# Every engine's loops written out in a transformer block with two routed FFN passes and one attention: constant waits, no branches

## The reference

```python
x = x + 0.5 * ffn(layernorm(x))
x = x + attn(layernorm(x))
x = x + 0.5 * ffn(layernorm(x))
```

## The kernel before, in words

| sequence | engines | before the loop | loop | behind it |
|---|---|---|---|---|
| s0 of a pass, 8 blocks | PE, ACT, DVE, SP | 1 | 3 times 2 | 1 |
| s1, 8 blocks | PE, ACT | 2 | 3 times 2 | 0 |
| s1, 8 blocks | SP | 1 | 3 times 2 | 1 |
| e, 16 blocks | PE, ACT, DVE, SP | 1 | 3 times 4 | 3 |
| attention, 38 steps | PE, ACT, DVE, POOL | 7 | 6 times 4 | 7 |
| layer norm, 8 blocks | POOL | 1 | 3 times 2 | 1 |
| scatter, 32 tiles | POOL | 3 | 14 times 2 | 1 |
| expert sums, 16 blocks | POOL | 1 | 3 times 4 | 3 |

## Time and profile before

### The profile page before, as it was taken

The page is one execution under the profiler, slowest core; times in us unless marked ns, Lnnn a source line. Parts: engine busy times, 40 slices in busy tenths (PEclk is TensorE's granted clock), DMA queues, the critical chain, the costliest instruction groups (busy, mean ns, idle before and its releaser), DMA issues. The chain is left out here.

```text
span 2445.0 us, 42873 instructions
## 1 busy us (share of the span) xinstructions
PE 2300.4 (94%) x14276; PEld 2116.3 (87%) x14276; DVE 1379.4 (56%) x2890; ACT 970.2 (40%) x1940; POOL 501.5 (21%) x614
## 2 busy tenths in 40 slices
PE   7999999998999997788888988999999998999997
PEld 6888888887999997688888877888888887999997
DVE  4554454433666666778777773554454433666663
ACT  3333333332444444545444542333333332544442
POOL 1000003442121122223222220000003443121222
PEclk9999999998999999778787787999999998999999
DMA  6212113422343443100000002212113422343441
GB/s 207 72 59 87 61 57 107 126 81 72 94 104 91 99 99 90 61 1 0 0 0 0 0 1 87 76 56 87 61 57 109 124 80 68 98 103 89 102 92 17
DMA packets 198241, 175.59 MB, mean 72 GB/s; under 512 B 18697, under 2 KB 176829, under 8 KB 198144
## 3 DMA queue, kind: packets, MB, share of 16 engines
q1 hardware_dynamic: 177152, 144.57, 19.4%
q0 software_dynamic: 20992, 29.77, 6.4%
HBM read 108.51 MB, written 72.26 MB: 74 GB/s over the span
## 5 line engine op out<-in xcount | busy, mean ns | idle before, releaser
L340 PE MATMUL gate_p<-zh,w 128*128 128x320 f32 (+1 forms) x2048 | 641.3, 358 | 3.3 <-DVE zl L845 3.3
L340 PE MATMUL quad<-zh,w 128*128 128x320 f32 (+1 forms) x2048 | 628.8, 352 | 0.0
L1032 DVE TENSOR_TENSOR h_s<-quad,sg_s 128x512 f32<-128x512 f32 (+1 forms) x512 | 302.2, 590 | 473.9 <-PE quad L340 467.0
L658 ACT CAST hh<-h_s 128x512 fp32r<-128x512 f32 (+1 forms) x512 | 276.4, 540 | 648.9 <-DVE h_s L1032 648.9
L1040 DVE TENSOR_TENSOR hl<-h_s,hh 128x512 fp32r<-128x512 f32 (+1 forms) x512 | 303.8, 593 | 305.1 <-ACT hh L658 305.1
L649 ACT ACTIVATE sg_s<-gate_p 128x512 f32<-128x512 f32 (+1 forms) x512 | 265.2, 518 | 414.7 <-PE gate_p L340 414.5
L377 PE MATMUL quad<-w,hh 128*128 128x256 f32 x2048 | 410.2, 283 | 3.9 <-DVE hl L1040 3.9
L340 PEld LDWEIGHTS quad<-zh,w 128*128 128x128 f32 x2048 | 375.6, 189 | 44.2
L340 PEld LDWEIGHTS gate_p<-zh,w 128*128 128x128 f32 x2048 | 377.5, 189 | 40.3 <-DVE zl L845 3.7
L340 PE MATMUL gate_p<-zl,w 128*128 128x512 f32 (+1 forms) x1024 | 361.7, 353 | 0.0
L340 PE MATMUL quad<-zl,w 128*128 128x512 f32 (+1 forms) x1024 | 360.0, 352 | 0.0
(11 more groups left out here) (179 smaller groups left out, 3002.1 us busy)
## 6 DMA issues: line engine op xcount, KB each, us to landing
stage<-in_L_ffn_rg SPq DMA_DIRECT2D x128, 128.0 KB, 2.3
stage<-in_L_ffn_ru SPq DMA_DIRECT2D x128, 128.0 KB, 2.4
stage<-in_L_ffn_rd SPq DMA_DIRECT2D x128, 128.0 KB, 2.3
slots_d<-empty SPq DMA_DIRECT2D x16, 662.5 KB, 4.8
xr<-slots_d SPq DMA_DIRECT2D x32, 265.0 KB, 3.0
zh_d<-zh SPq DMA_DIRECT2D x16, 512.0 KB, 3.1
zl_d<-zl SPq DMA_DIRECT2D x16, 512.0 KB, 3.9
zn_d<-zn SPq DMA_DIRECT2D x16, 512.0 KB, 5.1
```

Of the source, the lines that this page charges most:

```text
L340: last = pe.matmul(dst, a, b, start=(k == 0), stop=(k == 3 * n - 1))
L658: nc.scalar.copy(hh[:, par, 0:ncol], h_s[:, par, 0:ncol]).then_inc(sm["hh_done"], 1)
L1032: v.tensor_tensor(h_s[:, par, 0:ncol], up_p[:, par, 0:ncol], sg_s[:, par, 0:ncol], ALU.mult).then_inc(sm["h_done"], 1)
```

## The change

In `sweep` the number of passes of the hardware loop is set to 0. The branch `if count > 1` isn't taken any more, `done` stays at `head`, and the last loop of the function calls the body for all remaining blocks with a plain `Step`. Every value that `at` gives is then a Python number, every wait compares with a constant, every address in `x`, `rstd`, `table`, `slots_d` and the weights in memory is fixed, and there is no loop instruction in any engine's program. The order of the work on each engine, its buffers, tiles and semaphore counts (but for the sequencers' own `sp_step`, which SP counts only behind waits on registers) stay as they are. The programs get longer in memory: what was one loop body stands there three, six or fourteen times.

```diff
@@ -55,7 +55,7 @@
 
     for b in range(head):
         body(Step(b, period))
-    count = (n - head - tail) // period
+    count = 0
     done = head
     if count > 1:
         with eng.Fori(0, count) as i:
```

## The result

| | before | after |
|---|---|---|
| median of 7 runs, us | 2442.60 | 2453.47 |
| lowest and highest, us | 2438.70, 2446.58 | 2449.76, 2459.21 |
| ratio to before, 95% interval | | 1.0044 [1.0027, 1.0060] |
| span of the profiled execution, us | 2445.0 | 2457.5 (own time 2459.21) |

Slower by 0.44%, outside the range of 2437 to 2448.

A forecast was written before the change was run, and what follows sets the result against it. TensorE, its matmul row busy 94% of the span, was taken to bound the kernel. Terms -0.1 + 0 - 1.1 + 2.0 = +0.8 us on 2445.0, shifted by 2.8 to the runs' median, gave 2443.0 us, no change; range 2437 to 2448.

The forecast's parts named there:

- What bounds the kernel: TensorE, full in the FFN blocks; the attention hangs on chains between five engines; one long standstill comes before the experts.
- Branches on TensorE: Loop ends in the FFN: the queue covers each branch but for 0.02 us; -0.1 us, bounds -0.24 and 0.
- register waits in the FFN: FFN blocks, five engines: nothing more than the 0.02 us between looped and unrolled blocks, so 0.
- Rival 1: TensorE's 17 taken loop ends each fetch their target, some 1 us each: 17 us faster, 2425; chance 0.04.
- The scatter: POOL, L1307 to L1325: 0.05 us less per tile, 11 tiles in each of 2 passes: -1.1 us, bounds -5.6 and 0.
- the term of +2.0 for code loading: Scatter row loads wait behind added instruction fetches: +1.0 us per scatter, +2.0 in all, bounds 0 and +10.9.
- Rival 2: Scatter row loads issued ahead of SP's bursts: -7 us for one per scatter, -14 for two, 2428 to 2436; chance 0.05.
- Code loading elsewhere: Outside the scatter: loads that fetches could hold have slack, and in the attention nothing is loaded.
- Rival 3: Exposed code loading on TensorE, in attention or scatter: one in five of 65 fetches bare, +14 us, 2456; chance 0.07.
- The attention: Steps 7 to 30: neither loop end nor register form is on the chain; 0, bounds -0.5 to +0.5 us.
- rival 4: Attention, another clock rhythm from a shifted start: 24 steps at 14.1 us give 2421, at 15.4 give 2452; chance 0.04 each way.
- The range: 2437 to 2448 us: down to the no-change bound, one microsecond over it above for code loading; chance 0.76.

The follow-up runs named there:

- e8: The kernel before, unchanged, run again as a control beside the kernel before: median 2450.45 us, ratio 0.9990.
- e3: Against the kernel before, only the attention's step loop on ACT, DVE and POOL written out, TensorE keeping its loop: 2449.82 us, ratio 0.9998.
- e10: The kernel before, loops kept, with unread filler matmuls in each attention step: 2392.58 us, ratio 0.9756 to the kernel before.
- e13: The changed kernel measured again, on a further chip, against the kernel before: 2447.36 us, ratio 0.9989.
- e9: The changed kernel plus a DVE write of 96 zero columns ahead of the add of L1155: 2458.47 us, ratio 1.0024 to the kernel before.
- e14: The changed kernel plus a DVE write of 288 zero columns ahead of the add of L1155: 2439.36 us, ratio 0.9959 to the kernel before.

## Why the prediction was wrong, step by step

**What bounds the kernel.** Right: the full FFN blocks did not move (33.44 us for a shared block, 22.96 for an expert block), and the stage that the change altered is the attention, where TensorE's clock averages 0.81.

**Branches on TensorE, register waits in the FFN.** Right: the expert blocks over what was a back edge went from 22.98 to 22.96 us. Even that 0.02 can't be told apart from the rest: full expert blocks lie between 22.95 and 22.99 us in both kernels, back edge or none. Rival 1 falls with it, and nothing of its 17 us came. The rule that I had cited, the Trainium skill's (Runtime: NRT & Kernel Launch, section Instruction fetch mechanics), is about a branch whose target isn't held, and would make the changed kernel the faster one if the loops' targets weren't. From 440 to 590 us the loops had run without any fetch, so its condition wasn't met there, and written out the fetches rose from 55 and 42 to 114 and 72.

**The scatter.** A tile's way from row load to indirect DMA was to shrink by 0.05 us. From the landing of the row load to the first indirect DMA it shrank from 0.952 us (median of the looped tiles) to 0.877, so 0.075, in both passes. That would be -1.65 us for 22 tiles. In the trace of after the last tiles before the standstill are these (POOL's timeline, start, us, what, [idle before]).

```profile
573.42 0.60 POOL L1317 DMA_DIRECT2D srow<-zn_d  x1
...
576.98 1.63 POOL L1323 DMA_INDIRECT slots_d<-srow,sidx  x1 [2.65 <-issue]
...
579.88 0.60 POOL L1317 DMA_DIRECT2D srow<-zn_d  x1
...
583.17 1.00 POOL L1323 DMA_INDIRECT slots_d<-srow,sidx  x1 [2.09 <-DMA srow<-zn_d]
```

Tile for tile with the earlier trace rows: the first load's indirect DMA starts after 3.56 us in place of 3.35 and takes 1.63 us in place of 1.00, so the next row load comes 6.46 us behind this one in place of 5.63; the other tile takes 3.29 against 3.25. One small fetch falls between 576 and 577.5 us. But e8, with its loops and no fetch between 570 and 590 us, has an indirect DMA of 1.76 us at the same tile, and those over 1.15 us number 16 in before and 17 in after. So no run shows the term of +2.0 for code loading. The standstills were 8.88 and 10.57 us before and 9.65 and 9.43 after, 0.4 us shorter in sum, against +0.9 forecast (-1.1 + 2.0). That says little of either term, since the second one alone goes from 4.1 to 12.4 us over the profiles without filler there.

Rival 2 (row loads slipping in front) isn't what the change does: the standstills changed by about 1 us each, in opposite directions. But something of its size occurs by itself. In e3 and e10, whose scatter is looped, and in e13, where it is written out, the second pass's standstill is 5.2, 5.0 and 4.1 us. The scatter took 198 to 199 us there and 202 us or more in the others, and the second FFN was at least 2.8 us shorter than in any other profile.

**Code loading elsewhere.** Right at about nothing: TensorE's largest wait for "issue" went from 30.1 to 30.4 us, its longest from 1.0 to 1.4. That isn't written-out code either, since e3, where TensorE keeps its attention loop, has 30.4 and 1.4 too. Rival 3 gave 2456 and the result is near it, but its exposed fetches aren't there.

**The attention.** This is the step of the mechanism that failed: "neither the loop end nor the register form is on that chain", with 0 and bounds of -0.5 to +0.5. I had compared 13.0 us steps, in which nothing waits for the add of L1155, and two tens that both were looped: ten looped steps against ten looped steps say nothing of unrolled ones. The register form is on the chain in the pairs only, at 0.11 us a short step. Taken alone that too is a small gain. What the profile shows is of the kind of rival 4, another rhythm of the clock: "at 15.4 us they lose 9, 2452". The mean of the ten steps after is 15.35 us, the attention lost 9.65 and the median is 2453.5. It was right in kind; what sets it off is not a shifted start but a step shorter by 0.1 us, present in every profile that has pairs and DVE's attention loop written out (but for e9 and e14, which delay the add). That the size fits as well is luck: over the whole stage the mean step went from 14.58 to 14.89 us, not to 15.4, the same kernel profiled again had attentions from 453.46 to 461.23, and in three further comparisons the medians differed by -2.6 to +6.7 us. Its other half, 24 steps of 14.1 us, has no ground: 14.1 us is only the short step of a pair, and the pattern of four has a mean of 14.49. At 0.04 for this direction the rival had too little, on the argument that two equal tens show a rhythm firmly held. They show only what holds at that pair length.

**The range.** It rested on three runs within 3.9 us. 31 runs of the same kernel in one group spread over 14.6 us, and the medians of before go from 2442.6 to 2453.2 over the comparisons. That term was missing from the range altogether: the spread of the medians, 10.6 us, is as wide as the whole range that I gave (11). This is the step that failed for the number. Four of the five later medians of the unchanged kernel (2450.3, 2453.2, 2450.6 and 2449.9) lie above 2448 as well, so a kernel that did nothing at all would have left the range there.

## What to carry to other kernels

Where a stage hangs on chains between engines at a clock that goes up and down, compare looped and unrolled passes in every kind of step that occurs, not only in the commonest, and expect that a tenth of a microsecond may move the time either way: here a short step of 14.10 us in place of 14.21 went with longer rows of pairs, and one of 14.33 came with 0.4% less time. A difference below 0.5% between kernels of this kind wants repeats on several chips: one comparison of seven runs gave +0.44%, three of twelve averaged +0.03%. Holding the clock up with products that nobody reads in TensorE's idle time was worth 57 us (0.976), against 0.7 for the loops at a clock so held; the best version measured is either kernel with that filler (2392.6 with loops, 2393.2 without), and it beats both. Writing out loops whose branches and waits lay under full engines gave nothing that could be measured here, and cost little, though large code fetches rose from 55 to 114.

## What was unexpected of the hardware

- In these traces a register-computed address is worked out behind the wait that stands before its instruction: 57 to 75 ns in DVE's sequencer, and the instruction starts 144 to 163 ns after its operand in place of 36 to 38.
- The attention's steps fall in with the changes of the granted clock, whose falls lie 30.72 us apart there. In single profiles, pairs of 30.72 us (e9) went on to the end of the stage, those of 30.74 came four in a row at most, and those of 30.80 singly.
- A small write ahead of the add made the instruction behind the add start 278 ns after it in place of 341 (e9), so a delay put in at one instruction reached the chain by less than half.
- The time of a run goes with its mean granted clock at about 1.8 us for each 0.001, with identical code, over a spread of 14.6 us.
- 14 filler products of 240 columns in each step cost nothing that can be seen: steps of 13.0 us are as long as the shortest ones without them.
